# The layer normalisation of a 24-step kernel as scalar_tensor_tensor with a broadcast operand

## The reference

```python
def _layernorm(x, axis=-1, eps=1e-05):
    m = jnp.mean(x, axis=axis, keepdims=True)
    v = jnp.var(x, axis=axis, keepdims=True)
    return (x - m) / jnp.sqrt(v + eps)

x = x + 0.5 * _L0_ffn_ref(_layernorm(x, axis=-1), ...)
```

## Time and profile before

| | |
|---|---|
| time, median of 3 runs | 1323.66 us (1321.03 to 1324.83) |
| profiled execution: time | 1322.77 us |
| profiled execution: span, first to last instruction | 1321.0 us |
| PE, DVE, ACT, POOL busy | 87%, 68%, 41%, 50% of the span |
| mean granted TensorE clock | 0.950 of full speed |
| line 281 | 96 instructions on DVE |

### The profile page before, as it was taken

How to read it: one execution, slowest core, us unless ns; L and a number is a source line. 1 busy time by engine, 2 the same in 40 slices (tenths; PEclk the granted TensorE clock), 3 DMA queues, 4 the chain that set the end, 5 groups by cost and what they waited for, 6 DMA issues and landing times.

```text
span 1321.0 us, 21598 instructions
## 1 busy us (share of the span) xinstructions
PE 1152.2 (87%) x6681; PEld 982.4 (74%) x6681; DVE 895.1 (68%) x2247; ACT 547.1 (41%) x1225; POOL 660.7 (50%) x784
## 2 busy tenths in 40 slices
PE   5887467999789998998988989998599999999996
PEld 4766366877666787876776778787489998799995
DVE  4577777588878847567868864646765555656566
ACT  2354742210110223227857842322255555555552
POOL 5556816730443286873414458678453544344430
PEclk9898888999789999998998999999699999999998
DMA  5214021230001032222102212323111111111100
GB/s 163 66 54 143 20 88 56 85 95 1 1 0 29 15 97 84 90 85 49 44 13 49 61 48 90 95 84 120 48 40 32 40 31 34 40 41 32 40 8 32
DMA packets 31972, 74.07 MB, mean 56 GB/s; under 512 B 7136, under 2 KB 10464, under 8 KB 31456
## 3 DMA queue, kind: packets, MB, share of 16 engines
q1 hardware_dynamic: 29520, 70.43, 17.8%
q10 hardware_dynamic: 1872, 2.74, 0.6%
q0 software_dynamic: 512, 0.07, 0.0%
HBM read 63.64 MB, written 3.28 MB: 51 GB/s over the span
## 4 chain that ended last, share of the span: by engine, by line
PE 59%; DVE 23%; ACT 7%; issue 6%; POOL 4%; DMA 1%; DVEq 0%; POOLq 0%; ACTq 0%; SPq 0%
PE ps L227 18%; PE ps L229 17%; PE ps L228 17%; PE ps L1241 3%; DVE a_ptl L1265 3%; DVE a_p L1202 2%; DVE x L1001 2%; ACT a_p L1210 2%; ACT a_pth L1257 2%; DVE ffn_hl L702 1%; ACT ffn_hh L661 1%; DVE stats L264 1%; PE ps L327 1%; DVE xn L281 1%; PE ps L1026 1%
## 5 line engine op out<-in xcount | busy, mean ns | idle before, releaser
L1228 POOL TENSOR_SCALAR a_p<-a_p,small 128x128 f32<-128x128 f32 (+3 forms) x256 | 131.8, 532 | 265.3 <-DVE small L1219 265.2
L227 PE MATMUL ps<-xh,wh 128*128 128x512 f32 x480 | 198.7, 414 | 9.9 <-POOL wl L418 5.4
L228 PE MATMUL ps<-xl,wh 128*128 128x512 f32 x480 | 193.2, 403 | 0.0
L229 PE MATMUL ps<-xh,wl 128*128 128x512 f32 x480 | 193.2, 402 | 0.0
L1210 ACT ACTIVATE a_p<-a_p,small 128x128 f32<-128x128 f32 (+3 forms) x256 | 141.6, 554 | 70.2 <-DVE small L1202 69.8
L387 POOL TENSOR_TENSOR wl<-raw,wh 128x384 fp32r<-128x384 f32 (+2 forms) x120 | 157.8, 1315 | 10.0
L385 POOL TENSOR_SCALAR wh<-raw 128x384 fp32r<-128x384 f32 (+2 forms) x120 | 77.1, 643 | 153.5 <-PE ps L229 153.4
L1265 DVE TENSOR_TENSOR a_ptl<-ps,a_pth 128x384 fp32r<-128x384 f32 (+1 forms) x192 | 106.6, 596 | 61.5 <-ACT a_pth L1257 61.3
L661 ACT ACTIVATE ffn_hh<-ffn_hf 128x512 fp32r<-128x512 f32 x88 | 55.5, 631 | 187.3 <-DVE ffn_hf L696 121.1
L418 POOL TENSOR_TENSOR wl<-raw,wh 128x512 fp32r<-128x512 f32 x88 | 117.6, 1337 | 7.3
L227 PE MATMUL ps<-wh,ffn_hh 128*128 128x256 f32 x352 | 105.2, 299 | 18.5 <-DVE ffn_hl L702 18.5
(11 more groups left out here) (308 smaller groups left out, 3091.8 us busy)
## 6 DMA issues: line engine op xcount, KB each, us to landing
raw<-in_w SPq DMA_DIRECT2D x56, 448.0 KB, 3.3
raw<-in_w SPq DMA_DIRECT2D x32, 384.0 KB, 3.0
raw<-in_qk SPq DMA_DIRECT2D x16, 512.0 KB, 3.5
raw<-in_v SPq DMA_DIRECT2D x16, 256.0 KB, 2.7
delta_table<-d_back SPq DMA_DIRECT2D x4, 528.0 KB, 5.2
d_back<-delta_table ACTq DMA_DIRECT2D x2, 1024.0 KB, 6.3
a_sq<-a_qh SPq DMA_DIRECT2D x64, 32.0 KB, 2.0
a_sk<-a_kh SPq DMA_DIRECT2D x64, 32.0 KB, 2.0
```

What stands on the lines that cost most here:

```text
L227: pe.matmul(o, l[0], r[0], start=start, stop=False, skip_group_check=True)
L228: pe.matmul(o, l[0], r[1], start=False, stop=False, skip_group_check=True)
L229: return pe.matmul(o, l[1], r[0], start=False, stop=stop, skip_group_check=True)
L1228: g.tensor_scalar(pp, pp, h_inv[:, par, i:i + 1], 1.0, ALU.mult, ALU.mult).then_inc(sem("at_norm"), 1)
```

## The change

The four instructions of dve_norm become scalar_tensor_tensor: (x - mean) * rstd, the mean still a scalar per partition, rstd no longer a second scalar but a tensor operand, one element per partition read with a step of zero over the 256 columns. The second norm (line 298), the semaphores and everything else stay.

```diff
@@ -278,8 +278,9 @@
             if positive(2 * (u - 1)):
                 v.wait_ge(sem("ln_T"), 2 * (u - 1))
             for i in tiles:
-                v.tensor_scalar(xn[:, b, i, :], x[:, TT * b + i, :], mv[:, b, i, 0:1], rstd[:, b, i:i + 1],
-                                ALU.subtract, ALU.mult).then_inc(sem("ln_xn"), 1)
+                v.scalar_tensor_tensor(out=xn[:, b, i, :], in0=x[:, TT * b + i, :], scalar=mv[:, b, i, 0:1],
+                                       in1=rstd[:, b, i:i + 1].to_broadcast([P, D]), op0=ALU.subtract, op1=ALU.mult)\
+                    .then_inc(sem("ln_xn"), 1)
             if KIND[u] == LIN1 and tiles[-1] == TT - 1:
                 for i in range(TT):
                     v.wait_ge(sem("ln_xn"), TT * u + i + 1)
```

## The result

The changed kernel takes 1326.88 us (median of 20 runs, 1321.19 to 1331.33) against 1324.43 for the kernel before in the same session (20 runs, 1321.03 to 1326.73): ratio 1.0023, 95% interval 1.0012 to 1.0033, so 2.5 to 3 us slower. Forecast were 1316.5 us and 7.1 us faster. The range of 1308 to 1326 misses it too, by 0.9 us.

A forecast was written before the change was run, and what follows sets the result against it. TensorE was taken to bound the kernel, with VectorE setting the end in stretches. Terms -1.2 - 4.8 - 7.4 + 1.7 + 4.4 + 0.2 = -7.1 us, off the median 1323.66, gave 1316.5 us; range 1308 to 1326.

The forecast's parts named there:

- What bounds the kernel, and who meets whom: Whole kernel: TensorE busy 87%, VectorE sets the end in stretches; line 281's norms and POOL take turns.
- Price with POOL quiet: Norms with POOL quiet: +0.07 us each, from line 1146; 24 on the path make +1.7 us.
- Question 1: Norm behind POOL's MEMSET at 401.21: no wait with the new instruction; unit 11's norm gains 4.8 us.
- Question 2: Norm behind a reading POOL instruction: ends 0.28 us after it, where it was 0.14.
- Question 3: Who comes next, VectorE or POOL: VectorE keeps its turn; four norms end 1.47 us after the first POOL instruction.
- the streak: Norms beside POOL: four run through while POOL's next instruction is held some 1.3 us, as beside line 1146.
- unit 0: First norm: four instructions take 2.1 us instead of 3.33, and TensorE's first work hangs on the fourth: -1.2 us.
- units 19 and 20: Norms near 923.65 and the next unit's: four take about 2.5 us instead of 7.02 and 5.52: -7.4 us for both.
- the starving of POOL: Places where TensorE needs split weights (506, 578, 836, 908, 259.9): POOL held by the norms delays them: +4.4 us.
- rival A: Norms and POOL take turns as with line 895, no wait behind the MEMSET: -1.0 us, 1322.7; chance 0.25.
- T: Experiments' theory: turns stay, only the MEMSET wait goes; at most +1.4 us with POOL quiet, +1.5 to +2.5 beside reading POOL.
- B: Rival: turns, and the norm at 401.21 still waits for the MEMSET; nothing gained, +3.8 us, 1327.5; chance 0.12.

The follow-up runs named there:

- gate4: Kernel before, old instruction kept, with POOL's splits beside the norms of units 19 and 20 waiting until all four norms are done: 1315.74 us, ratio 0.9940.
- free_only: Kernel before with the new instruction only in the twelve units whose norm finds POOL quiet or writing: 1326.26 us, ratio 1.0023.
- u11_only: Kernel before with the new instruction in unit 11 alone: 1320.18 us, ratio 0.9968.
- busy_only: Kernel before with the new instruction only in the eleven units whose norm meets a reading POOL instruction: 1327.96 us, ratio 1.0038.

## Why the prediction was wrong

**What bounds the kernel, and who meets whom**: right. Each norm waits out one POOL instruction, and taking POOL away (gate4) gives 1.38 us for 7.02.

**Price with POOL quiet**, +0.07 each: right, four in 1.66. The Trainium skill's higher estimate (VectorE: DVE Perf Modes) of 133 ns does not hold here; the measurement decides. What it costs in all, +1.7, is too low by the middle of free_only (+3.0), but not outside its interval.

**Question 1**, no wait behind a MEMSET: right, 0.48 inside the MEMSET. The Trainium skill (SBUF — State Buffer, Who interferes with whom) has two SBUF inputs contend only with a reading POOL instruction, and the 0.48 agrees. The term, -4.8, has a part that is not a gain. Its 18 products took 5.84 us before (406.64 to 412.48), and the forecast let them run at 0.23 each, 4.2: the 1.65 between is the slow clock behind the wait, which comes back in unit 12 or 13. The path is 5.2 us shorter, and by the trace 3.6 of it are left; u11_only has -4.2 with an interval of 1.9 to 6.8.

**Question 2**, a tail of 0.28 behind a reading instruction: right, 0.29.

**Question 3** is the step that failed: "The new instruction has 1146's form and width, so I take the streak". In its place the runs showed turns. The norms took turns wherever they met a reading POOL instruction, also with 1146's operand widths, own waits and the reverse order of arrival. So the form did not decide, and seven pairs of turns stood against one place with a streak. Why line 1146 kept its turn there stays open. With the step fell unit 0 (-1.2, its four took 0.31 longer), units 19 and 20 (-7.4, they took 0.37 longer each) and the starving of POOL (+4.4; TensorE's wait at 508.47 grew by 0.18). Without the streak the forecast is rival A's -1.0.

**From A's -1.0 to +2.5**: unit 11 is 1.2 of it, 3.6 by the trace for 4.8 (the clock's 1.65, less 0.4 by which the path got shorter than forecast). Five tails at 0.2 each were twice that where the trace was measured (0.44 and 0.40), +1. The rest, about 1.3, is in free_only's and busy_only's excess over T and can't be told from their intervals of about 2.5 us to either side.

**The chances**: A had 0.25 against 0.45 for the streak, and even A's own price left no room for slower by 0.2%. The range needed B's end, 1327.5.

## What to carry to other kernels

When one instruction seems to win or lose a shared resource, count every place where such a pair meets before the nearest-looking one decides; one place with one outcome is a range, not a value. If VectorE's operation waits for POOL's, move or cut POOL's instruction first: two or three semaphore waits on POOL gave 0.6% and 0.8% with VectorE's code untouched, and an instruction in four pieces shortened the norm from 4.53 to 1.94 us. When TensorE's work behind a wait is priced, look at its pace there: products that run at the lower clock behind the wait are not gained with it. Here 4.7 and 5.2 us left the stretch, 1.65 of them came back in a later one, and what stayed was about the idle time itself.

## What the hardware showed that was not expected

- With turns, a chain of VectorE instructions behind POOL lasts as long as POOL's: the fourth of four ends 0.14 us (tensor_scalar) or 0.29 us (scalar_tensor_tensor) after the POOL instruction, whatever its own 0.41 or 0.48.
- The same scalar_tensor_tensor kept its turn at one place in 19 of 20 traces: a 128x256 tensor_tensor of POOL took 2.12 us for 0.72 there, and a 128x1024 one 3.74 for 2.33.
- TensorE's clock: behind a wait of 2.59 us the products ran at the lower level, 0.43 us apart for 0.23, in all fourteen traces with that wait (0.95 in the stretch). With the wait gone that stretch had 1.00 and unit 12 or 13 had 0.98 instead, in all six such kernels: some 1.65 us moved and were not saved.
- A MEMSET of 128x8 (65 ns) ahead of each tensor_scalar cost nothing: four in 1.40 us for 1.38.
